# Joining the half bursts of two channel tiles, and turning the maxima before the sums are spread, in a two-layer attention kernel

## The reference, cut to what matters

```python
x = x + _L0_conv_ref(_gn(x), ...)   # windows of 8x8 tokens, 16 heads of 16, cosine scores, bias, shifted mask
x = x + _L1_conv_ref(_gn(x), ...)   # 8 heads that look back, 8 that look ahead, over an image's 256 tokens
...
s = jnp.einsum('bhqe,bhke->bhqk', q, k) * scale
mask = i[:, None] <= i[None, :] if lookahead else i[:, None] >= i[None, :]
s = jnp.where(mask, s, jnp.finfo(s.dtype).min)
p = jax.nn.softmax(s, axis=-1)
return jnp.einsum('bhqk,bhke->bhqe', p, v)
```

## Time and profile before

| | |
|---|---|
| median of 3 runs | 1354.71 us (1350.8 to 1357.26) |
| the profiled execution | 1353.95 us, its span 1352.2 us |
| PE busy | 1261.8 us, 93% of the span |
| DVE busy | 819.2 us, 61% |
| ACT busy | 644.9 us, 48% |
| POOL busy | 200.5 us, 15% |
| mean granted TensorE clock | 0.977 |

### The profile page before, as it was taken

The page is one execution under the profiler, slowest core; times in us unless marked ns, Lnnn a source line. Parts: engine busy times, 40 slices in busy tenths (PEclk is TensorE's granted clock), DMA queues, the critical chain, the costliest instruction groups (busy, mean ns, idle before and its releaser), DMA issues.

```text
span 1352.2 us, 51651 instructions
## 1 busy us (share of the span) xinstructions
PE 1261.8 (93%) x21788; PEld 914.3 (68%) x21788; DVE 819.2 (61%) x1623; ACT 644.9 (48%) x1115; POOL 200.5 (15%) x272
## 2 busy tenths in 40 slices
PE   6699999999999999859999999999999999999996
PEld 2467676776777767636677777777777777777764
DVE  2488888788788887644555555555555454545431
ACT  2365555565566555403444444444444444444442
POOL 0001111111111111111121212121111111111120
PEclk9699999999999999979999999999999999999998
DMA  2000000000000000010112121211121212111213
GB/s 76 13 19 19 23 19 17 18 16 17 18 16 16 16 10 4 4 34 1 21 29 44 29 44 27 43 27 43 27 43 27 43 27 43 27 43 27 43 29 70
DMA packets 161781, 37.50 MB, mean 28 GB/s; under 512 B 136068, under 2 KB 160918, under 8 KB 161686
## 3 DMA queue, kind: packets, MB, share of 16 engines
q1 hardware_dynamic: 160632, 35.96, 12.2%
q10 hardware_dynamic: 1056, 0.13, 0.1%
HBM read 19.17 MB, written 16.78 MB: 27 GB/s over the span
## 4 chain that ended last, share of the span: by engine, by line
PE 54%; ACT 1%; DVE 0%; DMA 0%; issue 0%
PE psG L970 11%; PE psA L1043 8%; PE psA L1027 7%; PE psG L997 7%; PE psG L1006 6%; PE psE L1099 4%; PE psA L1055 4%; PE psG L982 3%; PE psA L1081 2%; PE psE L1067 1%; PE psE L1091 1%; ACT probs L1125 1%; DVE cm L1176 0%; DMA scratch_heads<-on 0%; DMA rows<-scratch_heads 0%
## 5 line engine op out<-in xcount | busy, mean ns | idle before, releaser
L1176 DVE TENSOR_REDUCE cm<-psG 128x4 f32<-128x1024 f32 (+1 forms) x256 | 245.2, 958 | 316.9 <-PE psG L1006 316.9
L1125 ACT ACTIVATE probs<-psG 128x1024 f32<-128x1024 f32 (+1 forms) x256 | 207.9, 812 | 229.4 <-PE psG L982 229.4
L997 PE MATMUL psG<-stack 32*128 32x256 f32 (+1 forms) x2048 | 238.1, 350 | 5.3 <-DVE cm L1176 4.1
L970 PE MATMUL psG<-stack 32*128 32x512 f32 (+1 forms) x1024 | 235.3, 536 | 7.9 <-ACT probs L1125 7.8
L1228 POOL TENSOR_SCALAR_AFFINE_SELECT probs<-probs 128x1024 f32<-128x1024 f32 x128 | 139.9, 1093 | 606.8 <-ACT probs L1125 606.8
L997 PEld LDWEIGHTS psG<-stack 32*128 32x128 f32 x2048 | 156.0, 185 | 13.1 <-DVE cm L1176 5.1
L443 PE MATMUL psA<-probs,xh 128*128 128x512 f32 x256 | 131.7, 642 | 9.3 <-ACT xh L562 5.3
L764 POOL TENSOR_TENSOR X<-X,probs 128x96 f32 (+5 forms) x128 | 55.0, 462 | 520.1 <-ACT probs L529 520.1
L1043 PE MATMUL psA<-xh,wqk 128*128 128x256 f32 x512 | 125.0, 388 | 5.6 <-DVE xh L1207 5.6
L970 PEld LDWEIGHTS psG<-stack 32*128 32x128 f32 x1024 | 77.0, 183 | 74.0 <-issue 57.8
L1043 PEld LDWEIGHTS psA<-xh,wqk 128*128 128x128 f32 x512 | 94.8, 195 | 18.0 <-DVE xh L1207 6.4
(11 more groups left out here) (137 smaller groups left out, 1995.1 us busy)
## 6 DMA issues: line engine op xcount, KB each, us to landing
X<-in_xr SPq DMA_DIRECT2D x32, 256.0 KB, 2.7
scratch_heads<-on SPq DMA_DIRECT2D x64, 128.0 KB, 3.0
rows<-scratch_heads SPq DMA_DIRECT2D x32, 256.0 KB, 3.0
out<-X SPq DMA_DIRECT2D x32, 256.0 KB, 2.2
probs<-in_wqk SPq DMA_DIRECT2D x1, 512.0 KB, 4.0
wv<-in_wv SPq DMA_DIRECT2D x2, 256.0 KB, 4.3
wqk<-in_wqk SPq DMA_DIRECT2D x1, 512.0 KB, 3.7
probs<-in_wo SPq DMA_DIRECT2D x1, 256.0 KB
```

The costliest lines, as they stand in the source:

```text
L970: nc.tensor.matmul(G[:, bank * 512:bank * 512 + 2 * b.size].rearrange("p (e q) -> p e q", e=2), kt[i.k][own_rows(r), o, b.keys_of * P:(b.k ...
L997: nc.tensor.matmul(G[:, at:at + b.size], qm[i.k][own_rows(r), o, e, b.queries_of * P:(b.queries_of + 1) * P], kt[i.k][own_rows(r), o, b.ke ...
L1125: nc.scalar.activation(weights[:, at:at + 4 * b.size].rearrange("p (r x) -> p r x", r=2), banks, ACT.Exp).then_inc(exp_done, 1)
L1176: nc.vector.reduce_max(cm[o][:, b.queries_of, :].rearrange("p (r x) -> p r x", x=COL)[:, first:first + 2, 0:2], banks.rearrange("p r (e k) ...
```

## The change

Two edits. In the first layer PE's list has `turn_c` ahead of `spread_sums`. In the second layer the halves of the two tiles are joined: a burst is now one of `WHOLE_0`, `WHOLE_0B`, `HALVES`, `HALVES_B`, `WHOLE_1`, `WHOLE_1B`, six for an image, each of 1024 columns for ACT and for DVE. The other stages are spread anew over the six gaps, the weights' storage is laid out anew, and the four masks of POOL wait for other exponentials.

```diff
@@ -465,8 +465,8 @@
                 nc.tensor.matmul(E[:, :], spread, rdx, start=True, stop=True).then_inc(spread_done, 1)
 
             pipeline(pe, images, [(scores, 0), (project_v, 1), (output, -1), (bounds, 1), (turn, 2), (sums, 0), (weigh, 0),
-                                  (lambda i: project(i, 0), 3), (groups, 4), (lambda i: project(i, 1), 3), (spread_sums, 0),
-                                  (turn_c, 1)], LAGS, once=(TABLE_STEP, prepare))
+                                  (lambda i: project(i, 0), 3), (groups, 4), (lambda i: project(i, 1), 3), (turn_c, 1),
+                                  (spread_sums, 0)], LAGS, once=(TABLE_STEP, prepare))
...
 class Burst:
 
 
-    def __init__(self, tile, n):
-        self.tile, self.n = tile, n
-        self.at = tile * BURSTS + n
-        self.whole = n < 2
+    def __init__(self, at, tile, n):
+        self.at, self.tile = at, tile
+        self.whole = tile is not None
+        self.tiles = (tile,) if self.whole else range(CT)
+        self.weigh_rows = (0, 1) if n == 0 else (2, 3)
+        self.bound_rows = (2, 3) if n == 0 else (0, 1)
         self.size = TOKENS if self.whole else P
...
+
+        self.weights_at = prob_at(tile, self.weigh_rows[0])
+
+    def keys_of(self, o):
+        return o if self.whole else 1 - o
+
+    def queries(self, o):
+        return slice(0, TOKENS) if self.whole else slice((1 - o) * P, (2 - o) * P)
+
+    def queries_of(self, o):
+        return 1 - o if self.whole else o
+
+    def keys(self, o):
+        return slice(0, TOKENS) if self.whole else slice(o * P, (o + 1) * P)
+
+    def column(self, o, e):
+        return e * TOKENS if self.whole else (o * 2 + e) * P
+
+
+def prob_at(tile, row):
+
+    return (4096 if tile is None else tile * 2048) + row * 512
+
+
+WHOLE_0, WHOLE_0B, HALVES, HALVES_B, WHOLE_1, WHOLE_1B = BURSTS = [
+    Burst(n, tile, n % 2) for n, tile in enumerate((0, 0, None, None, 1, 1))]
...
+    ALL = len(BURSTS)
+    HALF_DONE = HALVES_B.at + 1
...
+            def weigh_keys(i, b):
+
+                if b is HALVES:
+                    wait(pe, qk_out[1], i.count(QK_OPS[1]))
                 wait(pe, exp_done, i.count(ALL, b.at) if b.at else i.plus(-1).count(ALL))
+                for o in b.tiles:
                     for bank, r in enumerate(b.weigh_rows):
+                        at = bank * 512 + b.column(o, 0)
+                        nc.tensor.matmul(G[:, at:at + 2 * b.size].rearrange("p (e q) -> p e q", e=2),
+                                         kt[i.k][own_rows(r), o, b.keys_of(o) * P:(b.keys_of(o) + 1) * P],
+                                         qm[i.k][own_rows(r), o, :, b.queries(o)], start=(o == b.tiles[0]), stop=False,
+                                         skip_group_check=True)
+
+            def lower_by_bound(i, b):
+
+                if b is WHOLE_0:
+                    wait(pe, c_out[0], i.count(1))
+                if b is HALVES:
+                    wait(pe, c_out[1], i.count(1))
+                for o in b.tiles:
+                    for e in range(2):
+                        for bank, r in enumerate(b.weigh_rows):
+                            at = bank * 512 + b.column(o, e)
+                            last = nc.tensor.matmul(G[:, at:at + b.size], pick[own_rows(r), e, :],
+                                                    ct[o][own_rows(r), b.queries(o)], start=False, stop=True,
+                                                    skip_group_check=True)
+                            if e == 1 and o == b.tiles[-1]:
+                                last.then_inc(s_ready, 1)
+
+            def bound_queries(i, b):
+
+                if b is WHOLE_0:
+                    wait(pe, qk_out[0], i.count(QK_OPS[0]))
+                if b is HALVES:
+                    wait(pe, qk_out[1], i.count(QK_OPS[1]))
                 wait(pe, max_done, i.count(ALL, b.at) if b.at else i.plus(-1).count(ALL))
+                for o in b.tiles:
+                    for e in range(2):
+                        for bank, r in enumerate(b.bound_rows):
+                            at = (2 + bank) * 512 + b.column(o, e)
+                            nc.tensor.matmul(G[:, at:at + b.size],
+                                             qm[i.k][own_rows(r), o, e, b.queries_of(o) * P:(b.queries_of(o) + 1) * P],
+                                             kt[i.k][own_rows(r), o, b.keys(o)], start=(e == 0 and o == b.tiles[0]), stop=False,
+                                             skip_group_check=True)
+
+            def mask_bounds(i, b):
                 for bank in (2, 3):
+                    for o in b.tiles:
+                        at = bank * 512 + b.column(o, 0)
+                        scores = G[:, at:at + 2 * b.size].rearrange("p (e k) -> p e k", e=2)
+                        diagonal = (1 - o) * P if b.whole else 0
+                        last = nc.tensor.matmul(scores[:, :, diagonal:diagonal + P], identb[:, :],
+                                                (below if o else above)[:, :].unsqueeze(1).to_broadcast([P, 2, P]),
+                                                start=False, stop=True, skip_group_check=True)
                 last.then_inc(max_ready, 1)
...
-                wait(pe, masked, i.count(2 * CT, 2 * (o + 1)))
+                wait(pe, masked, i.count(4, 2 if o == 0 else 4))
...
...
-                wait(pe, max_done, i.count(ALL, BURSTS * (o + 1)))
+                wait(pe, max_done, i.count(ALL, ALL if o else HALF_DONE))
...
-            pipeline(pe, images, [*B(0, 0), (lambda i: project_qk(i, 1), 1),
-                                  *B(0, 1), (lambda i: weigh(i, 1), -1), (lambda i: turn_c(i, 1), 0),
-                                  *B(0, 2), (project_v, 1),
-                                  *B(0, 3), (lambda i: turn(i, 0), -1), (turn_rows, -3),
-                                  *B(1, 0), (output, -3),
-                                  *B(1, 1), (lambda i: project_qk(i, 0), 2),
-                                  *B(1, 2), (lambda i: turn(i, 1), -1), (lambda i: turn_c(i, 0), 1),
-                                  *B(1, 3), (lambda i: weigh(i, 0), 0)], LAGS)
+            pipeline(pe, images, [*B(WHOLE_0), (lambda i: project_qk(i, 1), 1),
+                                  *B(WHOLE_0B), (lambda i: turn_c(i, 1), 0), (lambda i: weigh(i, 1), -1),
+                                  *B(HALVES), (project_v, 1),
+                                  *B(HALVES_B), (lambda i: turn(i, 0), -1), (turn_rows, -3), (lambda i: project_qk(i, 0), 2),
+                                  *B(WHOLE_1), (output, -3), (lambda i: turn(i, 1), -1),
+                                  *B(WHOLE_1B), (lambda i: turn_c(i, 0), 1), (lambda i: weigh(i, 0), 0)], LAGS)
...
-            pipeline(act, images, [(lambda i: copy_outputs(i, 0), -1), X_(0, 0), X_(0, 1),
-                                   (lambda i: copy_outputs(i, 1), -1), (lambda i: copy_c(i, 1), 0), X_(0, 2), (copy_v, 1),
-                                   X_(0, 3), (copy_rows, -3), X_(1, 0), X_(1, 1), (copy_qk, 2), X_(1, 2),
-                                   (lambda i: copy_c(i, 0), 1), X_(1, 3)], LAGS)
+            pipeline(act, images, [(lambda i: copy_outputs(i, 0), -1), X_(WHOLE_0), X_(WHOLE_0B), (lambda i: copy_c(i, 1), 0),
+                                   (lambda i: copy_outputs(i, 1), -1), X_(HALVES), (copy_v, 1), X_(HALVES_B), (copy_rows, -3),
+                                   (copy_qk, 2), X_(WHOLE_1), X_(WHOLE_1B), (lambda i: copy_c(i, 0), 1)], LAGS)
...
+                if b.whole:
+                    slots = cm[:, b.tile, b.queries_of(b.tile), :].rearrange("p (r x) -> p r x", x=COL)[:, rows, 0:2]
+                    scores = banks.rearrange("p r (e k) -> p r e k", e=2)
+                else:
+                    slots = (cm[:, :, :, :].rearrange("p o t x -> p (o t) x")[:, 0::3, :]
+                             .rearrange("p o (r x) -> p r o x", x=COL)[:, rows, :, 0:2])
+                    scores = banks.rearrange("p r (o e k) -> p r o e k", o=2, e=2)
+                nc.vector.reduce_max(slots, scores, AX_X).then_inc(max_done, 1)
...
+            pipeline(dve, images, [R(WHOLE_0), (copy_qk, 1), R(WHOLE_0B), (normalize, 2), R(HALVES), R(HALVES_B),
+                                   (lambda i: divide(i, 0), -1), R(WHOLE_1), (residual, -3), (lambda i: divide(i, 1), -1),
+                                   R(WHOLE_1B)], LAGS)
...
-            pipeline(pool, images, [K(0, True), K(0, False), K(1, True), K(1, False)], LAGS)
+            pipeline(pool, images, [K(0, WHOLE_0B), K(0, HALVES_B), K(1, HALVES_B), K(1, WHOLE_1B)], LAGS)
```

More of the change, by code:

```diff
@@ L812, in layer1 @@
     above = sb("above", [P, P], BF16)
-    cm = [sb(f"cm1{o}", [P, TT, P]) for o in range(CT)]
+    cm = sb("cm1", [P, CT, TT, P])
     ct = [sb(f"ct1{o}", [P, TOKENS], BF16) for o in range(CT)]
@@ L974, in lower_by_bound @@
[L974 to L978, removed]
-                for e in range(2):
-                    for bank, r in enumerate(b.weigh_rows):
```

(26 more changed lines are left out.)

108 lines of the change are left out of this document (29 added, 79 removed).

## The result

| | before | after |
|---|---|---|
| median, 4 runs each | 1355.99 us | 1309.64 us (1303.17 to 1312.16) |
| ratio of the times | | 0.9639, 95% interval 0.9566 to 0.9712 |
| the profiled execution | 1353.95 us, span 1352.2 | 1312.16 us, span 1310.4 |
| median step of an image, first layer | 15.56 us | 14.98 us |
| step of an image, second layer | 22.46 us | 21.60 us |

The forecast was 1313 us; a second measurement of the changed kernel, beside the later experiments, gave 1314.35 us and a ratio of 0.968 (0.9641 to 0.9719). The steps in the table are read between the starts of the same stage in successive images.

What follows compares the result with a forecast made beforehand. PE's own stream was taken to bound the second layer; in the first, `scores` waited 18.3 us for ACT's copy. Gains of 15 and 26 us, 41 together, from 1353.95 gave 1313 us, range 1304 to 1328.

Steps and rivals of the forecast that it cites:

- What bounds the kernel: Second layer's steady stretch: only PE's own stream counts, busy 658.22 of 660 us; DVE and ACT about half.
- First layer: `turn_c` ahead of `spread_sums` starts ACT's copy earlier: 0.48 us a step, 15 us over 31 steps.
- The joined burst: Second layer: a joined burst takes 1.72 us against 1.96 for two halves, saving 0.48 us an image.
- Entries: Second layer: three fewer entries into row groups on PE at 0.10 us each, saving 0.30 us an image.
- Short waits: Second layer: wider gaps remove a half burst's wait for DVE to empty the banks, 0.05 us an image.
- Cover: Second layer: PE's work behind a joined burst outlasts DVE's reduction, 2.28 against 1.87 us, leaving at least 0.41.
- Filling and draining: Pipeline's start and end, where bursts wait for DVE or ACT: could give 1 to 3 us, counted as 0.
- Rival (a): Matmuls start in program order, so weighing delays a joined burst's bounds: 0.70 us an image lost, 1335 us; chance 0.07.
- (b): First layer gives nothing, the copy still last through ACT's queue or DVE's chain: 1328 us; chance 0.08.
- (c): Slower: DVE's joined reduction outlasts its cover; 2.3 us would give 1354, 2.5 us 1366; chance 0.02.
- (d): Nothing in sum: weighing and bounding fully serialised, 0.77 us lost a burst, 1361 at worst, around 1350; chance 0.04.

Runs made afterwards that it cites:

- two stretches: Changed kernel, PE running each joined burst as all four stages of tile 0's half, then tile 1's; ACT and DVE unchanged: 1318.37 us, ratio 0.9698.
- lowering first: Changed kernel with `lower_by_bound` ahead of `bound_queries` in every burst: 1345.83 us, ratio 0.9932.
- four lowerings first: Changed kernel with tile 0's four lowerings ahead of the bounds in joined bursts, tile 1's behind them: 1322.06 us, ratio 0.9755.
- the doubled reduction: Changed kernel with DVE's reduction of the burst `HALVES` made twice, the first into a spare tile: 1324.74 us, ratio 0.9777.
- the copy's own run: Changed kernel with ACT's copy of the maxima ahead of the second square in the first layer: 1311.25 us, ratio 0.9671.
- the repetition: Changed kernel unedited, measured again in another set: 1314.35 us, ratio 0.968.
- the first edit's excess: Kernel before with only the first layer's edit: 1333.34 us, ratio 0.9826; 23 us less, where 31 steps give 18.

## Why the prediction was right, by its own steps

**What bounds the kernel: right.** In the second layer each edit that changed PE's step moved the layer's phase with it: by 16.8 us (two stretches), 51.3 (lowering first), 20.3 (four lowerings first) and 16.7 (the doubled reduction, once it was beyond its cover). Leaving ACT's and DVE's instructions as in the changed kernel did not keep the gain. The times moved the same way, but by less.

**First layer: mechanism right, term too small.** 0.48 us a step was forecast, 0.59 came (0.585 as the mean of two steps). The queue on ACT was named rightly, but I let the copy start at the square's end, 0.60 us after the square's start; it starts 0.50 after it (303.70, 304.20). With that and the copy's delay to `scores` of 0.50, ACT's way takes 1.20 us and PE's own 1.17 (0.22 for the turning, 0.95 behind the spreading): the two end nearly together. In every second step the copy's delay is 0.10 longer, before the change as after it. What is late next is DVE, as the copy's own run showed: it has less than the square's 0.28 us of room in every second step. In the profiled execution only 12.9 of the 18 us appear. Between executions with equally many packets of instructions it is 16.3, twice; the changed kernel's has nine packets more than the one before, worth 3.5 us here (583.9 against 580.4), and the last 2 us are not accounted for.

**The joined burst: right, slightly high.** 1.72 us forecast, 1.73 measured; the two halves it replaces took 1.95, not 1.96. That is 0.43 us a step, where 0.48 was forecast. The lowering takes the whole burst's 0.32 (909.71 to 910.03), not two halves' 0.42. The run with two stretches shows the price itself, 0.31 a burst and 0.61 a step: 0.09 for one more entry, 0.10 each for one more weigh-and-bound and one more lowering, and 0.01 in the masks, whose number is the same.

**Entries: right.** 0.30 forecast, 0.28 came, as three times 0.093: `turn_rows` takes 0.44 instead of 0.53, `output` into `turn` 1.73 instead of 1.82, the two masks that stood before `weigh` each lose 0.09, and `turn` takes 0.09 more, since a burst now follows it.

**Short waits: term too small.** 0.05 was forecast, 0.155 came, 0.06 of it the late bounds of rows 5. The rest is `turn_c`, which took 0.37 and 0.35 us into a half burst and takes 0.31 into `weigh` now. In the kernel before, its own weight load waits for DVE's maxima at one of its two places (912.03), and at the other the burst behind it waits for ACT (903.10):

```profile
903.10 0.30 PEld L970 LDWEIGHTS psG<-stack 32*128 32x128 f32 x4 [0.21 <-ACT probs L1125]
...
912.03 0.20 PEld L1067 LDWEIGHTS psE<-ident,cm 128*128 128x128 f32 x2 [0.20 <-DVE cm L1176]
```

So the step's 0.86 is 0.43 + 0.28 + 0.155, and 0.83 was forecast as 0.48 + 0.30 + 0.05: the sum is closer than its terms.

**Cover: right.** 0.41 us forecast for a joined burst. The timeline leaves 0.42 from DVE's end to the next bounds, of which 0.06 is the way from a reduction's end to the bounds when they wait for it; the doubled reduction measured 0.37.

**Filling and draining** gave 3.2 us (0.5 and 2.7), counted as 0, with 3 in the range.

**The sum.** 41 us forecast, 41.8 in the profiled executions. That it is so close is partly luck. The first layer's 15 should have been 18 by its steps, and 12.9 appeared; the second's 26 was 3 too small, nearly all of it the filling and draining.

**Rival (a)** was wrong for this kernel, but not for the reason I gave in full. A stalled row group does not hold up another one as long as no more than eight passes stand ahead. The joined burst has exactly eight, four weighings of two passes; that it did was luck, since I knew of no limit: two more would have cost 0.27 us a step, eight more 1.57. The rule of the Trainium skill that I weighed ("TensorE: Matmul & The Clock Gate", "The mechanism"), strict program order, does not hold in these traces: in a whole burst with lowering first, the bounds start at 0.03 us and the four lowerings ahead of them at 0.96. Nor did my reading hold that a stalled group never holds another one.

**Rivals (b), (c), (d)** did not come: the first layer gave its gain, and the joined reduction takes 1.23 us, as the whole one.

## What to carry to other kernels

When PE is busy for 99% of a stretch, compare a long and a short burst of the same stages: what does not scale with columns is paid for each burst, and joining bursts saves it even though no matmul goes. Put matmuls that can run beside each other, in other row groups, close together in the queue; in this kernel no more than eight unfinished passes could stand ahead of them without a delay. A small stage whose result goes through another engine belongs ahead of the independent stage next to it, and then what is queued ahead of it on that engine is the next limit. Where another part of the kernel varies by itself, compare the phase that was edited and not the whole time.

## What the runs showed of the hardware that was not expected

**A look-ahead of eight passes** over unfinished matmuls in other row groups: bounds began at 0.03, 0.33, 0.55 and 0.98 us with 8, 10, 12 and 16 ahead. Matmuls and columns as what is counted are ruled out above; whether it is passes themselves or their weight loads was not told apart.

**The first layer's length varies with instruction fetches.** The DMA queue of instructions in the changed kernel (packets, MB, share of the span):

```profile
q8 instruction: 88, 1.44, 0.5%
```

and in the run with four of the lowerings ahead, whose first layer is the same code:

```profile
q8 instruction: 61, 1.00, 0.3%
```

With the changed kernel's first layer, in different profiled executions, it took 567.6 us with 88 packets (571.3 in the repetition and 569.6 with two stretches, 88 too), 565.9 and 564.1 with 79, 558.6 with 70, and 554.0 with 61, twice. The packets come nine at a time, some 95 us apart, while the loop runs; some 8 us after each group PE stands for 1.6 to 2.2 us inside `scores`, waiting for nothing but issue, and for 0.9 to 1.5 us more in `project_v` (L382) some 20 us later. The one inside `scores`:

```profile
322.83 0.83 PE L339 MATMUL psG<-stack 32*64 32x64 f32 x50 [1.91 <-issue]
```

and after most of these gaps the granted clock is at half (1.2 GHz) for 3.4 us, here from 323.4 us, after having been at 2.4 GHz since 71 us. That is 4.5 to 6 us for each group of nine (3.5 between the two kernels with the first layer as before), and 17 us between the shortest and the longest of these first layers, though some of the kernels differ only in the second. What sets the fetches off was not tried, and that they cause the gaps is argued from the times, not shown. It limits what a difference of 1% in this kernel's time can mean, and it may be where the first edit's excess comes from.
